# A paired cross-attention kernel: the order of the Grams, the scores and the attention product on TensorE, and what is put off by a step

## What is computed

```python
# layer 0: channel attention both ways, residuals added
heads = lambda t, w: (t @ w.T).reshape(b, n, 8, 16).transpose(0, 2, 1, 3)
def xca(q, k, v):
    attn = softmax(einsum('bhni,bhnj->bhij', q, k) * 16 ** -0.5)
    return einsum('bhnd,bhde->bhne', v, attn)        # then back to [b, n, 128]
rgb_att = rgb + xca(heads(rgb, wq_rgb), heads(geo, wk_point), heads(geo, wv_point)) @ proj_p2r.T
geo_att = geo + xca(heads(geo, wq_point), heads(rgb, wk_rgb), heads(rgb, wv_rgb)) @ proj_r2p.T
x1 = (rgb_att + geo_att).T                            # rgb = x.T, geo = y.T
# layer 1: q, k from y, v from x1, all with biases; group norm over a whole batch
scores = einsum('bhdl,bhel->bhde', q, k) / sqrt(128)
o = Wo @ (softmax(scores) @ v) + bo + x1
out = (o - mean(o)) * rsqrt(var(o) + 1e-5) * gn_w + gn_b
```

## Time and profile before

| | us |
|---|---|
| median of 3 runs | 351.15 |
| lowest, highest | 349.2, 351.64 |
| the profiled execution's own time | 351.63 |
| its span, first to last instruction | 349.7 |
| mean granted TensorE clock in it | 0.985 of full speed |

### The profile page before, as it was taken

The page is one execution under the profiler, slowest core; times in us unless marked ns, Lnnn a source line. Parts: engine busy times, 40 slices in busy tenths (PEclk is TensorE's granted clock), DMA queues, the critical chain, the costliest instruction groups (busy, mean ns, idle before and its releaser), DMA issues.

```text
span 349.7 us, 8291 instructions
## 1 busy us (share of the span) xinstructions
PE 335.8 (96%) x2678; PEld 281.5 (80%) x2678; DVE 230.7 (66%) x649; ACT 251.5 (72%) x410; POOL 188.9 (54%) x277
## 2 busy tenths in 40 slices
PE   6999999999999999999999999999999999999980
PEld 3788888797888889788888979888887988887760
DVE  2365694848668494866759485675948576692864
ACT  2546787778778787778878777887878787786332
POOL 0673892754819184572919467390937639092010
PEclk9899999999999999999999999999999999999995
DMA  7937566566575746556585656648575661203014
GB/s 232 382 119 243 178 201 186 205 214 236 179 275 180 274 148 219 201 189 255 180 275 177 247 174 192 254 146 272 180 221 185 199 242 49 120 0 122 0 43 200
DMA packets 29643, 66.39 MB, mean 190 GB/s; under 512 B 2368, under 2 KB 16960, under 8 KB 29632
## 3 DMA queue, kind: packets, MB, share of 16 engines
q1 hardware_dynamic: 25600, 51.57, 45.6%
q10 hardware_dynamic: 4032, 14.68, 10.7%
HBM read 49.47 MB, written 16.78 MB: 189 GB/s over the span
## 4 chain that ended last, share of the span: by engine, by line
PE 92%; DVE 3%; issue 2%; DMA 1%; ACT 1%; SPq 0%; POOLq 0%; POOL 0%
PE gacc L359 33%; PE oacc L379 9%; PE oacc L384 8%; PE oacc L380 8%; PE tpx L316 7%; PE mid L469 4%; PE mid L403 4%; PE mid L446 4%; PE mid L455 2%; PE mid L406 2%; PE mid L456 2%; DMA raw<-in_ctx 1%; PE mid L458 1%; PE mid L457 1%; PE mid L416 1%
## 5 line engine op out<-in xcount | busy, mean ns | idle before, releaser
L1013 POOL TENSOR_TENSOR xy_lo<-raw,xy_hi 128x256 fp32r<-128x256 f32 x256 | 177.8, 733 | 128.3 <-ACT xy_hi L631 128.3
L359 PE MATMUL gacc<-t 128*128 128x257 f32 x512 | 126.2, 389 | 0.8 <-ACT t L563 0.8
L359 PEld LDWEIGHTS gacc<-t 128*128 128x128 f32 x512 | 93.4, 192 | 14.8 <-issue 2.6
L631 ACT ACTIVATE xy_hi<-raw 128x1024 fp32r<-128x1024 f32 x64 | 67.1, 1051 | 0.0
L783 DVE STREAM_TRANSPOSE t<-y_blocks 128x512 f32<-128x512 f32 x56 | 64.5, 1152 | 0.0
L379 PE MATMUL oacc<-xy_hi,pq_hi 128*128 128x512 f32 x124 | 51.9, 419 | 0.4 <-ACT pq_hi L610 0.2
L380 PE MATMUL oacc<-xy_lo,pq_hi 128*128 128x512 f32 x124 | 48.9, 395 | 0.0
L563 ACT ACTIVATE t<-tpx 128x512 f32<-128x512 f32 x64 | 38.0, 597 | 9.3 <-PE tpx L329 8.4
L638 ACT ACTIVATE res<-oacc 128x512 f32<-128x512 f32 x60 | 35.7, 595 | 11.6 <-PE oacc L384 9.9
L794 DVE BATCH_NORM_STATS2 hstat<-res 128x6 f32<-128x512 f32 x60 | 39.4, 676 | 6.2 <-ACT res L638 6.2
L384 PE MATMUL oacc<-xy_hi,pq_lo 128*128 128x512 f32 x124 | 39.0, 395 | 0.0
(11 more groups left out here) (116 smaller groups left out, 427.3 us busy)
## 6 DMA issues: line engine op xcount, KB each, us to landing
raw<-in_x SPq DMA_DIRECT2D x31, 512.0 KB, 7.8
raw<-in_ctx SPq DMA_DIRECT2D x31, 512.0 KB, 9.4
y_blocks<-in_ctx SPq DMA_DIRECT2D x112, 128.0 KB
out<-res ACTq DMA_DIRECT2D x28, 512.0 KB, 6.4
out<-res SPq DMA_DIRECT2D x4, 512.0 KB, 2.6
wt<-in_weights SPq DMA_DIRECT2D x1, 896.0 KB, 6.8
raw<-in_x SPq DMA_DIRECT2D x2, 256.0 KB, 4.1
raw<-in_ctx SPq DMA_DIRECT2D x2, 256.0 KB, 5.2
```

The lines of the kernel that those rows point to most:

```text
L359: mm = pe.matmul(gacc[:, 0:2 * C + 1], t[slot][:, c, C:2 * C], t[slot][:, c, :], start=(c == 0), stop=(c == CH - 1))
L631: act.activation(xy_hi[slot][:, s, :], raw[slot][:, s, :], ACT.Copy).then_inc(split_hi, 1)
L1013: piece = pool.tensor_tensor(xy_lo[slot][:, s, cols], raw[slot][:, s, cols], xy_hi[slot][:, s, cols].bitcast(f32), ALU.subtract)
```

## The change

- `steps`: steps 2 and 3 are unrolled too, and the loop runs from step 4 to 15. Every step gets a flag `post`, false up to step 2.
- PE: P and Q of a pair, and its norm statistics, are formed a step later (`pq_products(p-2)`, `group_moments(p-3)`, near the start of a step). In the loop the order is: transposes, P and Q, u12, statistics, first output half, u3, transposes of batch 1, second half, scores, both Grams, z, the two halves of batch 1, M. The wait for the attention weights stands ahead of the last chunk of the second Gram.
- The Grams of the two batches have a bank each, `gacc` and the upper part of the bank `stat`; both banks are zeroed at the start. The columns of t and gram are now [y, ones, x] in place of [x, y, ones]; the width stays 257. Before the second Gram PE waits for `var_ready`, after which the statistics in `stat` are no longer in use.
- `load_blocks`: four DMAs by destination quadrant (32 partitions, 4 KB each) in place of four by column block (128 partitions, 1 KB each).
- VectorE's statistics of a pair's batch 1, its moments, `pq_low` and `variance` stand at the start of the next step, ahead of the y transposes; `abv` is formed ahead of `attn`; POOL's last `split_low` and `deviation`, and ACT's last `split_high`, move to the next step.

```diff
-        mean_s, abv_s = stat[:, 16:18], stat[:, 32:34]
+        mean_s, abv_s = stat[:, 16:18], mid0[:, 12 * W32:12 * W32 + 2]
+        gacc_b = [gacc[:, 0:GW], stat[:, H64:H64 + GW]]
...
-                blocks = y[4 * h + n].rearrange("(i c) (a m) -> i a c m", c=W32, a=QUADS)
-                for i in range(QUADS):
-                    sp.dma_start(y_blocks[n][:, i, :], blocks[i]).then_inc(blocks_in[n], 16)
+                blocks = y[4 * h + n].rearrange("(i c) (a m) -> a c i m", c=W32, a=QUADS)
+                for a in range(QUADS):
+                    sp.dma_start(y_blocks[n][W32 * a:W32 * (a + 1), :, :], blocks[a]).then_inc(blocks_in[n], 16)
...
-                if begin == 0 and not (isinstance(n, int) and n < 1):
-                    pe.wait_ge(gram_ready, n)
+                if begin == 0 and not (isinstance(n, int) and n < 2):
+                    pe.wait_ge(gram_ready, n - 1)
                 for c in range(begin, end):
-                    mm = pe.matmul(gacc[:, 0:2 * C + 1], t[slot][:, c, C:2 * C], t[slot][:, c, :],
-                                   start=(c == 0), stop=(c == CH - 1))
+                    first, final = c == 0, c == CH - 1
+                    mm = pe.matmul(acc, tb[:, c, 0:C], tb[:, c, :], start=first, stop=final)
```

TensorE in steps 0 and 1 (the second transposes of batch 1 and the second half of its Gram follow as before):

```diff
-                    gram_chunks(h, u, 0, 0, 4)
                     x_transpose_early(1, 0)
                     y_transpose_early(1, 0)
+                    pe.wait_ge(banks_zero, 2)
+                    gram_chunks(h, u, 0, 0, 4)
                     gram_chunks(h, u, 0, 4, 8)
...
                     z_operands(p - 1)
+                    gram_chunks(h, u, 1, 4, 5)
                     z_products(p - 1)
-                    gram_chunks(h, u, 1, 0, 4)
+                    gram_chunks(h, u, 1, 5, 8)
                     m_products(p - 1, False)
-                    gram_chunks(h, u, 1, 4, 6)
-                    pq_products(p - 1)
-                    gram_chunks(h, u, 1, 6, 8)
```

More of the change, by code:

```diff
@@ L15 @@
 W32 = 32
+XC = C + 1
+GW = XC + C
 TB = 4
@@ L193, in steps, with before @@
         def steps(eng, step):
[L194 to L200, removed]
+            step(0, 0, True, False, False, False)
+            step(0, 1, True, True, False, False)
+            step(1, 0, True, True, True, False)
+            step(1, 1, True, True, True, True)
+            with eng.Fori(2, PAIRS // 2) as i:
+                step(i, 0, True, True, True, True)
+                step(i, 1, True, True, True, True)
+            step(PAIRS // 2, 0, False, True, True, True)
+            step(PAIRS // 2, 1, False, False, True, True)
+        def before(h, u):
+            return (h - 1, 0) if u == 1 else (h - 2, 1)
         BOTH = slice(0, 2)
@@ L471, in pq_products, with step @@
                 mm.then_inc(pq_done, 1)
-            def step(h, u, front, middle, back):
+            def step(h, u, front, middle, back, post):
                 p = 2 * h + u
@@ L681, in step @@
                     xt_out(h, u, 1, 0)
                     xt_out(h, u, 1, 1)
+                    if post:
+                        normalise(*before(h, u), 0)
+                    out_to_sbuf(h - 1, u, 0, 1)
+                    if post:
+                        normalise(*before(h, u), 1)
+                    exponent(p - 1)
+                    if post:
+                        store(*before(h, u), 0)
+                    split_high(h, u, 0, 0, back)
+                    if post:
+                        store(*before(h, u), 1)
@@ L965, in step @@
                     c_out(p - 1, 1 - u)
-                    pq_low(p - 1, 1 - u)
                 elif middle:
+                    half_stats(*before(h, u), 1, 0)
+                    half_stats(*before(h, u), 1, 1)
+                    half_moments(p - 3)
+                    partition_moments(p - 3, 1 - u)
+                    pq_low(p - 2, u)
+                    variance(p - 3, 1 - u)
                     u3_out(p - 1)
@@ L1020, in deviation, with step @@
                 pool.tensor_tensor(rstd[:, bs], var[:, bs], neg_half[:, bs], ALU.pow).then_inc(rstd_ready, 1)
-            def step(h, u, front, middle, back):
+            def step(h, u, front, middle, back, post):
                 p = 2 * h + u
+                if front and middle and post:
+                    deviation(p - 3)
+                if middle and back:
+                    split_low(h - 1 + u, 1 - u, 1, 1)
                 if front:
@@ L1027, in step @@
                     split_low(h, u, 1, 0)
-                if back and (front or middle):
+                    if not middle:
+                        split_low(h, u, 1, 1)
+                elif middle:
+                    deviation(p - 3)
                     deviation(p - 2)
-                elif back:
+                else:
                     for b in range(2):
                         deviation(p - 2, slice(b, b + 1))
-                if front:
-                    split_low(h, u, 1, 1)
             steps(pool, step)
```

179 lines of the change are left out of this document (90 added, 89 removed).

## The result

The changed kernel takes 361.37 us (median, 360.79 to 361.88), the kernel before 351.14 in the same comparison (349.2 to 351.64): a ratio of 1.032, 95% interval 1.029 to 1.035. The forecast was 358.0 with a range of 352.5 to 364.5: slower as said, inside the range, but at the upper edge of the forecast's own 355.5 to 361.5. The span of the profiled executions grew by 9.3 us (349.7 to 359.0) where 7.2 was forecast. In later comparisons the kernel before has medians of 349.4 to 350.5 and the changed kernel 361.6, so the change costs 10 to 12 us; why before's own time spreads is in the part on the start.

The account below looks back on a forecast made before the run. PE's own list of work was taken to bound the kernel; start +0.4, loop wait +4.6 and step 16 +2.2 sum to +7.2, taken as 358.0 us. The forecast's own range was 355.5 to 361.5, 8 in 10 352.5 to 364.5.

Parts of the forecast that it names:

- What bounds it, and the sign: Whole kernel: PE's own work bounds the loop, reordering alone wins nothing there; 2% slower, chance of slower 0.73.
- hand-overs: PE in the loop: switches between kinds of matmul cost the same in their new pairs, 0.20, 0.26, 0.11, 0.11; change zero.
- Rival (b): Loop: Gram behind scores and output behind z cost no hand-over, 14 steps lose 6.4 us; 347 us, chance 0.08.
- Rival (a): Loop: VectorE meets PE in time, so no wait at the statistics matmul; 353.4 us, chance 0.17.
- rival (c): Loop: attention weights or a refill late; half a us more per step 364.5, one us 371; chance 0.15.
- The new wait on PE in the loop: Statistics matmul waits for VectorE's moments, 0.35 us in each of 13 loop steps: +4.6 us.
- The bound of 0.7 for the wait: Loop: largest wait per step at the statistics matmul, if recorded durations, not overlapped starts, count.
- In step 0 ... I expect the clock low: Unrolled start: low clock for four to eight Gram chunks; +0.9 taken, bounds -0.9 and +2.3; start sum +0.4.
- Steps 1 and 2: Unrolled start: step 1 +0.45, with P and Q out and M nearer z; step 2 lacks the statistics, -0.1.
- Step 16: Unrolled end: u3 ends 4.2 us into the step against 2.0 before: +2.2, bounds +1.3 and +3.
- What follows ... is the same chain: Step 16 behind u3: halves, z, M, P and Q, last outputs and statistics unchanged, so nothing added.
- What was late next: Loop: with the wait for the moments gone, `pq_low` would be the next late condition; no size given.

Follow-up runs that it names:

- e2: Changed kernel with one of the two output statistics moved into VectorE's idle time ahead of n12: 354.69 us, ratio to before 1.015.
- e3: Changed kernel with POOL's rstd ahead of its low-part pieces in step 16: 360.01 us, ratio to before 1.031.
- e1: Changed kernel with the loop's statistics matmul moved behind the first output half: 357.32 us, ratio to before 1.023.
- c2: Changed kernel with one statistic early, rstd first in step 16, step 0's old order and four output waits ahead of the statistics matmul: 355.9 us, ratio 1.016.
- e10: Changed kernel with the first output half's four waits issued ahead of the statistics matmul: 359.64 us, ratio to before 1.028.
- e8: Kernel before with only the block loads changed, to loads by quadrant: 349.95 us, ratio to before 0.999.
- e9: Kernel before with step 0's second Gram split into two calls of four chunks: 350.08 us, ratio to before 0.998.
- e6: Changed kernel with the block loads by column again: 361.30 us, ratio to before 1.031.

## Why the prediction was right and wrong

**What bounds it, and the sign: right.** PE's list was the time, the reordering took nothing off it, and every new wait showed in full. The hand-overs came to zero as taken: scores to Gram 0.24, z to output 0.19, M's end to a transpose 0.10 and statistics to output 0.11 (as read from an unrolled step; in the loop it is more, see below) make 0.64, where the old four made 0.68. Rival (b), the faster one, needed these to vanish. Rival (a) needed VectorE in time; it is late by more, not less. Of rival (c) nothing came in the loop: no loads, no attention weights are late there. The forecast's sign for (c), a period above 20.8, would have misled: the period is 20.79 with the room intact.

**The new wait on PE in the loop: mechanism right, term mis-sized.** VectorE's 3.35 measured 3.40 and PE's 3.32 measured 3.31. The sum of 0.33 to 0.35 was for a step like that one, where 0.41 was measured. It left out two things. In every second step, the one behind the jump back of the loop, VectorE's chain is 0.22 longer, so it waits 0.64. And "statistics to output (0.34 against 0.23, so 0.11)" was read from an unrolled step: there it holds (0.33 to 0.34 in step 3 and at the end), in the loop this hand-over measured 0.50 to 0.53, with the four waits ahead of it. That part isn't the wait for the moments, for it stays in e2. Together 0.53 + 0.17 - 0.04 for the hand-overs = 0.66, against the 0.61 measured and the 0.35 taken; the 0.05 between is within what modelled ends can say. The bound of 0.7 for the wait held.

**"In step 0 ... I expect the clock low": wrong, +0.4 forecast, about -2.8 measured.** I took low clock behind an idle time to be the rule of this start, from one row. (The term has a slip too: 0.9 less at full clock and 1.4 or 2.8 more are +0.5 or +1.9, not the taken +0.9 and the bound +2.3.) The changed kernel's first Gram ran its 16 instructions in 3.65 us, so at full clock, right behind idle times of 0.72 and 0.67. So the clock's 1.4 came back instead of going, together with the 0.83 wait, which I hadn't seen (the rows quoted for step 0, end before it). The wait for the data of batch 1, which was in the sum, took part of that back. Since starts with the same code differ by 0.7 and more, part of the miss is chance. Steps 1 and 2 were right to 0.2.

**Step 16: "What follows ... is the same chain": this failed.** Up to u3 the sum held (4.26 against 4.1). What follows wasn't the same chain, because the moved statistics bring a rstd and a norm into step 16, and there POOL's order has `deviation` behind both splits, unlike in the loop. Of the 2.1 us over the forecast e3 gives back 1.6; the remaining half a microsecond was not taken apart (ACT still waits 1.06 for rstd in e3, ahead of its copy).

**What was late next.** `pq_low` was named. e1, e2 and c2 show the four waits of the first output half instead, of which `pq_high`, on ACT, is the latest, in the changed kernel done 0.3 to 0.5 us before the moments. How much of their cost is its lateness no run shows.

The total was 3.4 off (2.1 in the span of the profiled executions) only because the start's miss of 3.2 in the one direction covered the larger part of the loop's 3.2 and the end's 2.1 in the other. The 358.0 was not earned by its parts.

## What to carry to other kernels

Where one engine is busy 99% of a loop, as here, putting work off by a step gained nothing and made its producer's queue part of the bound: sum that queue from what releases it to what is asked for, and move anything else in it (here a statistic of 0.68 us) into the idle time ahead of the release. Do the same for every unrolled step, on every engine, since the order there is often another one. Count the waits that stand ahead of the next matmul too, take the price of a hand-over from a step of the same form (loop or unrolled), and look for the second latest condition before removing the latest.

## What was not expected of the hardware

- Waits cost time in the loop even where nothing waits long. With four of them right ahead of it, the first output matmul ended 0.50 to 0.53 us behind the statistics matmul, whether that one had been late (changed) or not (e2: 0.48 to 0.52); with the same four further ahead 0.33 (e10). In the unrolled step 3, where they compare with constants, it was 0.34 with the four in place. That the sequencer has no lead there is my reading; which of the four waits costs, and how much of it is `pq_high`, was not tried.
- Behind the jump back of the loop VectorE's chain is 0.22 us longer, though the engine waited for nothing that the profile shows. Of that 0.14 lies right behind the jump; the rest also stands in step 4, which no jump precedes, so the jump is not the whole reason.
- The start is not one number: eight Gram instructions took 3.13 us in one profile (the kernel before), 2.42 in another (e8) and 1.74 in a third (e9) with the same order, and u12 of step 1 spread over 0.7 us with the same code.
- VectorE's 128x128 scaling of a weight took 0.22 us in the changed kernel and 0.76 in e9, with POOL at work beside it in e9 alone; that POOL is the reason wasn't tested.
- The old block loads kept 3.3 packets in flight and the new ones 9.6, at no cost and no gain in time, in either kernel (e6, e8).
